# A two-layer attention kernel on one core: the first norm at other slots, its eps addition on GpSimd, and the minima transposed at full width

## The chip, the cores and the metric

The kernel runs on one NeuronCore of a Trainium2 chip. Times are device microseconds of one launch. The engines are TensorE (PE; PEld is its weight load), VectorE (DVE), ScalarE (ACT), GpSimd (POOL) and SyncE (SP), which here only issues DMAs. Each runs its own instruction list in order, and they meet at semaphores.

## What is computed

The reference is two cross-attention layers on x of 16 batches x 256 tokens x 256 features, which the kernel runs as three passes of attention:

```python
# layer 0 (pass 0)
tgt1 = _layer_norm(tgt, g1, be1)                       # eps 1e-5
tgt = tgt + _self_attn(tgt1, mask, ...)                # 16 heads of 16, additive mask
tgt = tgt + (memory @ Wg.T + bg)
tgt1 = _layer_norm(tgt, g2, be2)
x = tgt + (jax.nn.relu(tgt1 @ W1.T + b1) @ W2.T + b2)
# layer 1 (passes 1 and 2)
y = layer_norm(x, ln1_s, ln1_b)                        # eps 1e-6
x = mha(y, y, ..., causal=True) + x                    # pass 1
y = layer_norm(x, ln2_s, ln2_b)
y = mha(y, encoded, ..., causal=False) + x             # pass 2
z = layer_norm(y, ln3_s, ln3_b)
out = y + (jax.nn.relu(z @ mlp_w1 + mlp_b1) @ mlp_w2 + mlp_b2)
```

## The kernel before

A task is one batch in one pass; there are 48. The program is a software pipeline of steps; `steps` unrolls the edges of each pass and loops over pairs of steps within. In step s every engine goes through 16 slots (one for each head), and in each slot it does the parts of several tasks: `st.cur` (task s, whose scores are made), `st.prev`, `st.old` (earlier ones: output projection, MLP) and `st.nxt`, `st.nxt2` (later ones: q, k and v; the first norm). The order of an engine's work is that of the `if h == ...` lines in its `slot` function. Nothing else sets it, so an engine that waits in one place holds all that stands below.

The parts that matter here, for one step:

- **First norm** of the task two steps on: VectorE takes the statistics of `x_in` in slot 9 (L864), aggregates them and adds eps in slot 10 (L871, L874), GpSimd raises to the power -0.5 (L1095), VectorE normalises in slot 12 (L878), and TensorE transposes in slot 13 (L444).
- **q and k** of the next task are split into three bf16 parts. ScalarE writes the first part and the value (slots 3, 4), GpSimd subtracts (`q_f` slot 4, `k_f` slot 5; L1031 is the line of every subtraction), VectorE casts the second part (L914 slot 5, L917 slot 6), GpSimd makes the third (`q_part` slot 5, `k_part` slot 6). SP then writes the parts to DRAM (L381, L390) and reads them back as `q_stack` and `k_stack` (L399, L404). TensorE's score products of the next step need both stacks.
- **Scores.** TensorE makes the score product of head h in slot h (L494); it needs VectorE's guard of head h - 2. The guard (L858, in pass 2 L843) takes the minimum over the keys, and in passes 0 and 1 adds the bias on the way.
- **Minima** in passes 1 and 2: `top_split` on GpSimd splits the minima of four heads into bf16 parts (`top_part`, 12 columns), and TensorE transposes them with a 12-column weight at tile position (0, 96) (L521), in slots 2, 6, 10 and 14. ScalarE copies the rows into `q_stack` (L729), and `keyed_scores` (L542) uses them.
- **MLP** in passes 0 and 2, of task s - 2: four chunks of w1 on TensorE (slots 5 to 8), `h_f` on ScalarE (L805, slots 6 to 9), `h_hi` on VectorE (L921, slots 7 to 10), `h_lo` on GpSimd (slots 7 to 10). `h_f` of chunk 3 waits for `h_hi` and `h_lo` of chunk 1, that of chunk 4 for those of chunk 2. TensorE's V product (slot 10) waits for the last `h_f`, since it writes the same PSUM bank.
- **Norm of the attention output** (`rden`, `o_n`; L885, L890) in slot `NORM_AT` of VectorE, which is 6 in pass 0 and 10 in the others, then `o_f`, `ot_hi`, `ot_lo` one slot later.

In GpSimd's `slot` the power stands at the end of slot 10. Since eps is an immediate, the addition on VectorE is a `tensor_scalar`.

## Time and profile before

| | |
|---|---|
| median of 3 runs | 1709.86 us (1702.79 to 1710.65) |
| profiled execution | 1704.09 us, span 1702.3 us |
| mean granted TensorE clock | 0.956 |
| busy, share of the span | PE 86%, PEld 69%, DVE 71%, ACT 62%, POOL 49% |
| steady step of pass 0, of pass 2 | 38.5 to 40.1 us, 34.1 us |
| steps of pass 1 (766.90 to 1144.70) | 14 in 377.8 us |
| mean of one instruction | guard L858 0.42 (two for a head), copy of prob_t 0.68, h_lo 1.30, k_part subtraction 1.16, o_n 0.68, h_f 0.48 (two) |

A timeline row has the start, the duration, the engine, the line, the operation, what it writes and reads, and in brackets the idle time of that engine just before it and what ended it. "L494 PE" is line 494 of the kernel on TensorE.

### The profile page before, as it was taken

The numbers are of one execution on the slowest core, as the hardware profiler recorded it, in microseconds if no ns is written. First come the engines' busy times: TensorE is split into PE (matmuls) and PEld (weight loads), VectorE is DVE, ScalarE is ACT, GpSimd is POOL, SyncE is SP. The second block draws the span as 40 slices with busy tenths as digits, with TensorE's granted clock in tenths as the row PEclk, the third lists the DMA queues.
The fourth block names the chain that finished last, engine by engine and source line by source line (L and its number), as shares of the span: only waits on it lengthen the run. The fifth ranks groups of instructions, "written<-read, shape, count | busy, mean of one in ns | idle before, by whom it ended". The sixth has DMA issues, their size and how long they took to land.

```text
span 1702.3 us, 42833 instructions
## 1 busy us (share of the span) xinstructions
PE 1459.5 (86%) x13376; PEld 1175.9 (69%) x13376; DVE 1212.1 (71%) x3855; ACT 1061.9 (62%) x2153; POOL 834.7 (49%) x1125
## 2 busy tenths in 40 slices
PE   2789999999998998878787777778999999999986
PEld 1567788877777887765566555555777777777756
DVE  2688887888878887656666766666776777677742
ACT  3677676777777775445565555556656665666552
POOL 3345454444444566544344443444555655565533
PEclk8799999999999999989899999998999999999989
DMA  5645555444544455444655646574644364546300
GB/s 145 139 113 119 108 109 118 99 99 105 117 100 99 105 125 130 119 107 107 124 121 111 129 101 140 115 153 93 119 112 105 99 128 99 105 101 129 79 26 13
DMA packets 163511, 185.75 MB, mean 109 GB/s; under 512 B 15952, under 2 KB 140240, under 8 KB 163408
## 3 DMA queue, kind: packets, MB, share of 16 engines
q1 hardware_dynamic: 163408, 184.57, 49.8%
q8 instruction: 41, 0.67, 0.2%
q14 instruction: 62, 0.51, 0.1%
HBM read 125.78 MB, written 58.72 MB: 108 GB/s over the span
## 4 chain that ended last, share of the span: by engine, by line
PE 42%; issue 13%; ACT 12%; DVE 12%; DMA 9%; POOL 6%; SPq 5%; ACTq 1%; DVEq 0%; POOLq 0%
PE d_ps L437 16%; PE d_ps L673 8%; DMA k_stack<-parts 7%; PE o_ps L572 5%; PE s_ps L494 5%; PE t_ps L542 3%; DVE prob L858 3%; PE t_ps L508 3%; SPq L399 2%; DMA parts<-q_part 2%; ACT prob_t L721 2%; SPq L404 2%; DVE o_n L890 2%; POOL h_lo L1031 2%; PE m_ps L444 1%
## 5 line engine op out<-in xcount | busy, mean ns | idle before, releaser
L721 ACT ACTIVATE prob_t<-t_ps 128x384 f32<-128x384 f32 (+1 forms) x512 | 275.4, 551 | 393.0 <-PE t_ps L542 197.7
L494 PE MATMUL s_ps<-k_stack,q_stack 96*128 96x256 bf16 (+1 forms) x1536 | 294.6, 275 | 124.5 <-DMA k_stack<-parts 47.5
L712 ACT ACTIVATE prob<-prob,neg_max 128x256 f32<-128x256 f32 x512 | 233.8, 514 | 121.0 <-DVE neg_max L858 118.8
L494 PEld LDWEIGHTS s_ps<-k_stack,q_stack 96*128 96x128 bf16 x1536 | 115.1, 100 | 227.8 <-issue 65.7
L542 PE MATMUL t_ps<-q_stack,k_stack 108*128 108x256 bf16 (+1 forms) x1024 | 207.3, 269 | 23.0 <-ACT prob_t L721 14.3
L858 DVE CUSTOM_DVE_ANT_0 prob<-s_ps,bias_sb 128x256 f32<-128x256 f32 x512 | 192.4, 416 | 48.5 <-PE s_ps L494 36.7
L858 DVE CUSTOM_DVE_ANT_0 prob<-s_ps,causal 128x128 f32<-128x128 f32 (+1 forms) x512 | 158.5, 352 | 90.2 <-PE s_ps L494 88.0
L843 DVE TENSOR_REDUCE top<-s_ps 128x2 f32<-128x512 f32 x256 | 172.9, 682 | 54.8 <-PE s_ps L494 51.3
L1031 POOL TENSOR_TENSOR h_lo<-h_f,h_hi 128x512 fp32r<-128x512 f32 x128 | 165.9, 1296 | 86.6 <-DVE h_hi L921 86.6
L572 PE MATMUL o_ps<-prob_t,v_sb 128*17 128x256 f32 (+1 forms) x3072 | 200.7, 381 | 0.0
L437 PE MATMUL d_ps<-x2t_hi,w_hi 128*128 128x256 f32 x512 | 157.0, 307 | 38.2 <-ACT k_f L780 21.8
L901 DVE STREAM_TRANSPOSE o_q<-o_ps 128x256 f32<-128x256 f32 x192 | 86.1, 449 | 133.0 <-PE o_ps L572 131.4
L508 PE MATMUL t_ps<-ident_sb,prob 128*128 128x128 f32 x1024 | 160.3, 280 | 2.5 <-DVE prob_t L994 2.0
L673 PE MATMUL d_ps<-w_hi,h_hi 128*128 128x256 f32 x512 | 148.0, 289 | 4.4 <-POOL h_lo L1031 4.4
L673 PE MATMUL d_ps<-w_hi,h_lo 128*128 128x256 f32 x512 | 147.5, 288 | 0.0
L673 PE MATMUL d_ps<-w_lo,h_hi 128*128 128x256 f32 x512 | 146.4, 286 | 0.1
L437 PE MATMUL d_ps<-x2t_lo,w_hi 128*128 128x256 f32 x512 | 145.7, 285 | 0.0
L437 PE MATMUL d_ps<-x2t_hi,w_lo 128*128 128x256 f32 x512 | 145.4, 284 | 0.0
L729 ACT ACTIVATE q_stack<-o_ps 12x1024 bf16<-12x1024 f32 x128 | 130.1, 1016 | 11.5 <-PE o_ps L521 6.7
L437 PEld LDWEIGHTS d_ps<-x2t_hi,w_hi 128*128 128x128 f32 x512 | 98.8, 193 | 52.4 <-issue 44.1
L508 PEld LDWEIGHTS t_ps<-ident_sb,prob 128*128 128x128 f32 x1024 | 121.8, 144 | 14.0 <-issue 6.6
L1031 POOL TENSOR_TENSOR x2t_lo<-tf_b,x2t_hi 128x512 fp32r<-128x512 f32 x32 | 40.9, 1277 | 181.8 <-ACT tf_b L736 181.8
(115 smaller groups left out, 4063.5 us busy)
## 6 DMA issues: line engine op xcount, KB each, us to landing
q_stack<-parts SPq DMA_DIRECT2D x288, 128.0 KB, 4.0
k_stack<-parts SPq DMA_DIRECT2D x288, 128.0 KB, 6.4
parts<-q_part SPq DMA_DIRECT2D x96, 192.0 KB, 2.3
parts<-k_part SPq DMA_DIRECT2D x96, 192.0 KB, 2.3
ct_kept<-ct_hl SPq DMA_DIRECT2D x16, 512.0 KB, 8.0
x_in<-x_mid SPq DMA_DIRECT2D x32, 256.0 KB, 2.9
x_res<-x_mid SPq DMA_DIRECT2D x32, 256.0 KB, 3.0
ct_hl<-ct_kept SPq DMA_DIRECT2D x16, 512.0 KB, 8.2
```

The lines of the kernel that those rows point to most:

```text
L437: last = mm(dst, lhs, rhs, start=(opens and n == 0), stop=(closes and n == len(terms) - 1))
L494: last = mm(s_ps[:, h % 2, q * S:q * S + n], q_stack[0:ROWS, t.par, HEAD[h], q * P:(q + 1) * P], k_stack[0:ROWS, t.par, HEAD[h], 0:n], sta ...
L508: last = nc.tensor.transpose(t_ps[:, h % 2, c:c + P], prob[:, h % 4, q, k * P:(k + 1) * P], ident_sb[:, :])
L542: last = mm(t_ps[:, h % 2, k * S:k * S + S - lo], k_stack[:, t.par, HEAD[h], k * P:(k + 1) * P], q_stack[:, t.par, HEAD[h], lo:S], start=T ...
L572: last = mm(o_ps[32 * j:32 * j + VW, lo:S], v_sb[:, t.par, k, HEAD[h], :], prob_t[:, h % 8, k * S:k * S + S - lo], start=(k == 0), stop=(k ...
L673: last = mm(d_ps[:, 0, t * D:(t + 1) * D], lhs, rhs, start=(f == 0 and n == 0), stop=(f == FT - 1 and n == 2))
L712: last = nc.scalar.activation(prob[:, h % 4, q, :], prob[:, h % 4, q, :], ACT.Exp, bias=neg_max[:, h % 4, q:q + 1], scale=-1.0)
L721: nc.scalar.activation(prob_t[:, h % 8, 0:n], t_ps[:, h % 2, 0:n], ACT.Exp, scale=-1.0)\
L729: nc.scalar.activation(rows, o_ps[ROWS:ROWS + TOP, S:2 * S].unsqueeze(1).to_broadcast([TOP, CH, S]), ACT.Copy).then_inc(top_row.sem, 1)
L843: v.tensor_reduce(top[:, h // CH % 2, :, h % CH], s_ps[:, h % 2, :].rearrange("p (q k) -> p q k", q=TT), AX_X, ALU.min).then_inc(u_done.se ...
L858: last = v.tensor_tensor_reduce(prob[:, h % 4, q, 0:n], s_ps[:, h % 2, q * S:q * S + n], bias, 1.0, HUGE, ALU.add, ALU.min, least)
L1031: g.tensor_tensor(dst, a, b, ALU.subtract).then_inc(done, 1)
```

## The change

1. The statistics of the first norm go from slot 9 to slot 4, the aggregation from 10 to 5, and the normalisation from 12 to 6. The power on GpSimd goes with the aggregation, to the end of slot 5.
2. eps is added on GpSimd by a two-input addition against a tile of constants (`eps_sb`), for the first norm and the second. GpSimd waits for `ln_mv` (`ln2_mv`) in place of VectorE.
3. In pass 0 `NORM_AT` goes from 6 to 7.
4. The three parts of the minima are written to columns 96 to 107 of `top_wide`, whose other columns are zero, and transposed as a weight of 108 columns with no tile position.
5. The causal bias keeps one strip of 256 columns, from which both query tiles read a window.

```diff
-NORM_AT = (6, 10, 10)
+NORM_AT = (7, 10, 10)
+STATS_AT, MEAN_AT, HAT_AT = 4, 5, 6
...
-        top_part = sb("top_part", [P, 2, TT, CH, NSPLIT], BF16)
+        top_wide = sb("top_wide", [P, 2, TT, ROWS + TOP], BF16)
...
-                    last = mm(o_ps[ROWS:ROWS + TOP, S + q * P:S + (q + 1) * P],
-                              top_part[:, c % 2, q].rearrange("p j n -> p (j n)"), ident_bf[:, :],
-                              start=True, stop=True, tile_position=(0, ROWS))
+                    last = mm(o_ps[0:ROWS + TOP, S + q * P:S + (q + 1) * P], top_wide[:, c % 2, q, :], ident_bf[:, :],
+                              start=True, stop=True)
...
-                    bias = causal[:, q, 0:n] if t.p == 1 else bias_sb[:, t.par, q, 0:n]
+                    bias = causal[:, S - n:S] if t.p == 1 else bias_sb[:, t.par, q, 0:n]
...
                 last.then_inc(mv_done.sem, 1)
-                dve.wait_ge(mv_done.sem, mv_done.after(task))
-                v.tensor_scalar(ve_t[:, :], mv_t[:, :, 1], eps, None, ALU.add).then_inc(ve_done.sem, 1)
...
-                if h == 9 and has(st.nxt2):
+                if h == STATS_AT and has(st.nxt2):
...
-                if h == 10 and has(st.nxt2):
+                if h == MEAN_AT and has(st.nxt2):
...
-                if h == 12 and has(st.nxt2):
+                if h == HAT_AT and has(st.nxt2):
...
             g.memset(zeros[:, :, :], 0.0).then_inc(zeroed, 1)
-            pool.wait_ge(zeroed, 1)
+            g.memset(top_wide[:, :, :, :], 0.0).then_inc(zeroed, 1)
+            for p in range(NPASS):
+                g.memset(eps_sb[:, p], LN_EPS[p]).then_inc(zeroed, 1)
+            pool.wait_ge(zeroed, 2 + NPASS)
...
-                if h == 10 and has(st.nxt2):
+                if h == MEAN_AT and has(st.nxt2):
+                    pool.wait_ge(ln_mv.sem, ln_mv.after(st.nxt2))
+                    pool.sem_inc(passed, 1)
+                    g.tensor_tensor(ve[:, :], mv[:, :, 1], eps_sb[:, st.nxt2.p], ALU.add).then_inc(ln_ve.sem, 1)
...
                 if h == 14 and has(st.prev, MLP):
+                    pool.wait_ge(ln2_mv.sem, ln2_mv.after(st.prev))
+                    pool.sem_inc(passed, 1)
+                    g.tensor_tensor(ve2[:, :], mv2[:, :, 1], eps_sb[:, st.prev.p], ALU.add).then_inc(ln2_ve.sem, 1)
```

GpSimd in slots 5 to 8 of a step of pass 0, before (the names in brackets are the semaphores that an instruction waits for: `k_p2` counts VectorE's cast of k_part, `h_h` that of h_hi):

```order
L1031 TENSOR_TENSOR k_f<-k_f,k_part 128x512 [waits k_done]
L1031 TENSOR_TENSOR q_part<-q_f,q_part 128x512 [waits q_p2]
L1031 TENSOR_TENSOR k_part<-k_f,k_part 128x512 [waits k_p2]
L1074 REGISTER_ALU
L1031 TENSOR_TENSOR ct_hl<-tf_b,ct_hl 128x512 [waits ct_f]
L1078 REGISTER_ALU
L1031 TENSOR_TENSOR h_lo<-h_f,h_hi 128x512 [waits h_h]
```

and after:

```order
L1033 TENSOR_TENSOR k_f<-k_f,k_part 128x512 [waits k_done]
L1033 TENSOR_TENSOR q_part<-q_f,q_part 128x512 [waits q_p2]
L1095 REGISTER_ALU
L1097 TENSOR_TENSOR ve<-mv,eps_sb 128x2 [waits ln_mv]
L1101 TENSOR_TENSOR rstd<-ve,minus_half 128x2 [waits x_hat,ln_ve]
L1033 TENSOR_TENSOR k_part<-k_f,k_part 128x512 [waits k_p2]
L1077 REGISTER_ALU
L1033 TENSOR_TENSOR ct_hl<-tf_b,ct_hl 128x512 [waits ct_f]
```

The addition and the power now stand between the third parts of q and k.

VectorE in slots 5 to 7 of a step of pass 0, before (the ISA rows are guard 5, and below the cast guard 6):

```order
L914 CAST q_part<-q_f 128x512 [waits q_r]
L841 REGISTER_ALU
L858 ISA prob,neg_max<-s_ps,bias_sb 128x256 [waits s_mm,t_mm]
L858 ISA neg_max 128x1
L858 ISA prob,neg_max<-s_ps,bias_sb 128x256
L858 ISA neg_max 128x1
L885 RECIPROCAL rden<-o_q 128x32 [waits o_done]
L890 TENSOR_TENSOR o_n<-o_q,rden 128x2x8x16 [waits ot_f,rden_done]
L890 TENSOR_TENSOR o_n<-o_q,rden 128x2x8x16
L917 CAST k_part<-k_f 128x512 [waits k_r]
L841 REGISTER_ALU
L858 ISA prob,neg_max<-s_ps,bias_sb 128x256 [waits s_mm,t_mm]
```

and after, from the cast of k_part on:

```order
L916 CAST k_part<-k_f 128x512 [waits k_r]
L877 TENSOR_SCALAR x_in<-x_in,mv,rstd 128x256 [waits ln_rstd]
L877 TENSOR_SCALAR x_in<-x_in,mv,rstd 128x256
L842 REGISTER_ALU
L859 ISA prob,neg_max<-s_ps,bias_sb 128x256 [waits s_mm,t_mm]
L859 ISA neg_max 128x1
L859 ISA prob,neg_max<-s_ps,bias_sb 128x256
L859 ISA neg_max 128x1
L993 COPY prob_t<-t_ps 128x512 [waits t_mm]
L884 RECIPROCAL rden<-o_q 128x32 [waits o_done]
L889 TENSOR_TENSOR o_n<-o_q,rden 128x2x8x16 [waits ot_f,rden_done]
L889 TENSOR_TENSOR o_n<-o_q,rden 128x2x8x16
```

The normalisation, with its wait for `rstd`, stands ahead of guard 6, and the norm of the attention output behind it.

## Rows read from the trace of the kernel before

**Rows 1.** Stretches of one step, pass 0 and pass 2 (columns as in the first line).

```profile
core 0: us, PE busy (x) PEld busy (x) DVE busy (x) ACT busy (x) POOL busy (x), PEclk, DMA share, GB/s
461.50:500.00 38.50, 35.75 (x330) 31.08 (x328) 32.59 (x107) 28.43 (x67) 19.24 (x17) 1.00 0.53 109
1311.40:1345.50 34.10, 32.07 (x291) 25.41 (x290) 24.52 (x50) 21.88 (x42) 19.57 (x30) 1.00 0.41 108
```

**Rows 2.** Waits of TensorE in pass 1: total, times, longest.

```profile
PE s_ps L494 <- DMA k_stack<-parts: 35.2, 15, 4.4
```

**Rows 3.** Instructions that write `ve` or read it: ns min/median/max.

```profile
L874 DVE TENSOR_SCALAR ve<-mv x80: 169/170/1204, 8.5 to 1677.0; 128x2 f32<-128x2 f32 x80
L1095 POOL TENSOR_TENSOR rstd<-ve,minus_half x48: 688/690/708, 8.8 to 1573.9; 128x2 f32<-128x2 f32 x48
```

**Rows 4.** Timeline of GpSimd in a step of pass 0.

```profile
475.46 1.34 POOL L1031 TENSOR_TENSOR q_part<-q_f,q_part 128x512 bf16<-128x512 f32 x1
477.17 1.17 POOL L1031 TENSOR_TENSOR k_part<-k_f,k_part 128x512 bf16<-128x512 f32 x1 [0.37 <-DVE k_part L917]
478.29 1.30 POOL L1031 TENSOR_TENSOR ct_hl<-tf_b,ct_hl 128x512 fp32r<-128x512 f32 x1
```

**Rows 5.** Timeline of VectorE in the same step.

```profile
474.39 1.39 DVE L890 TENSOR_TENSOR o_n<-o_q,rden 128x256 f32<-128x256 f32 x1
475.70 1.39 DVE L917 CAST k_part<-k_f 128x512 bf16<-128x512 f32 x1
477.01 0.41 DVE L858 CUSTOM_DVE_ANT_0 prob<-s_ps,bias_sb 128x256 f32<-128x256 f32 x1
```

**Rows 6.** Timeline of GpSimd and VectorE at the end of that step.

```profile
499.49 1.27 POOL L1031 TENSOR_TENSOR xt_lo<-tf_a,xt_hi 128x512 fp32r<-128x512 f32 x1
...
500.17 1.07 DVE L878 TENSOR_SCALAR x_hat<-x,mv,rstd 128x256 f32<-128x256 f32 x2
```

**Rows 7.** Timeline of ScalarE in that step, the last h_f.

```profile
484.13 0.84 ACT L805 ACTIVATE h_f<-d_ps,cols_sb 128x256 f32<-128x256 f32 x2 [0.78 <-POOL h_lo L1031]
```

**Rows 8.** Timeline of TensorE in that step: score product 8, and V.

```profile
479.93 0.39 PE L494 MATMUL s_ps<-k_stack,q_stack 96*128 96x256 bf16 x2
...
485.02 0.38 PE L437 MATMUL d_ps<-w_hi,xt_hi 128*128 128x256 f32 x1 [0.45 <-ACT h_f L805]
```

**Rows 9.** Timeline of GpSimd in pass 1, a small addition.

```profile
994.51 0.20 POOL L1045 TENSOR_TENSOR top_rest<-top,top_part 128x8 f32<-128x8 f32 x1
```

**Rows 10.** Timeline of SP in the same step of pass 1.

```profile
994.37 0.93 SPq L390 DMA_DIRECT2D parts<-k_part  x2
995.71 2.66 SPq L399 DMA_DIRECT2D q_stack<-parts  x6
```

**Rows 11.** Timelines of four engines in a step of pass 2.

```profile
1322.07 1.37 DVE L914 CAST q_part<-q_f 128x512 bf16<-128x512 f32 x1 [1.03 <-POOL q_f L1031]
...
1324.88 0.68 DVE L843 TENSOR_REDUCE top<-s_ps 128x2 f32<-128x512 f32 x1
...
1325.04 1.16 POOL L1031 TENSOR_TENSOR k_part<-k_f,k_part 128x512 bf16<-128x512 f32 x1 [0.36 <-DVE k_part L917]
...
1330.45 0.84 ACT L805 ACTIVATE h_f<-d_ps,cols_sb 128x256 f32<-128x256 f32 x2
...
1336.49 0.39 PE L494 MATMUL s_ps<-k_stack,q_stack 96*128 96x256 bf16 x2 [0.40 <-DVE top L843]
```

**Rows 12.** Timeline of TensorE in that step, around a top product and V.

```profile
1331.05 0.39 PE L542 MATMUL t_ps<-q_stack,k_stack 108*128 108x256 bf16 x2
1331.27 0.38 PE L494 MATMUL s_ps<-k_stack,q_stack 96*128 96x256 bf16 x2
1331.59 0.28 PE L521 MATMUL o_ps<-ident_bf,top_part 128*12 128x128 bf16 x2
1331.79 0.39 PE L437 MATMUL d_ps<-w_hi,ct_hl 128*128 128x256 f32 x1
```

**Rows 13.** Weight loads by line: ns min/median/max.

```profile
L521 PEld LDWEIGHTS o_ps<-ident_bf,top_part x256: 83/87/93, 665.7 to 1651.6; 128*12 128x12 bf16 x128
L494 PEld LDWEIGHTS s_ps<-k_stack,q_stack x1536: 95/98/152, 41.3 to 1648.3; 96*128 96x128 bf16 x192
```

More of the change, by code:

```diff
@@ L176, in two_layers @@
         stats2, mv2, rstd2 = sb("stats2", [P, TT, 6]), sb("mv2", [P, TT, 2]), sb("rstd2", [P, TT])
+        eps_sb = sb("eps_sb", [P, NPASS, TT])
         ve, ve2 = sb("ve", [P, TT]), sb("ve2", [P, TT])
@@ L209, in two_layers @@
         bias_sb = sb("bias_sb", [P, 2, TT, S])
-        causal = sb("causal", [P, TT, S])
+        causal = sb("causal", [P, S])
         s_ps = es.enter_context(nc.psum_tensor("s_ps", [P, 2, 512], F32))
@@ L865, in statistics, with aggregate @@
                 last.then_inc(done.sem, 1)
-            def aggregate(task, st_t, mv_t, ve_t, eps, stats_done, mv_done, ve_done):
+            def aggregate(task, st_t, mv_t, stats_done, mv_done):
                 dve.wait_ge(stats_done.sem, stats_done.after(task))
@@ L936, in slot @@
                         dve.wait_ge(ln_rstd.sem, ln_rstd.after(st.nxt))
-                    aggregate(st.nxt2, stats, mv, ve, LN_EPS[st.nxt2.p], ln_stats, ln_mv, ln_ve)
+                    aggregate(st.nxt2, stats, mv, ln_stats, ln_mv)
                 if h == V_AT + 1 and has(st.nxt):
@@ L974, in slot @@
                         dve.wait_ge(ln2_rstd.sem, ln2_rstd.after(st.old))
-                    aggregate(t, stats2, mv2, ve2, LN_EPS[t.p], ln2_stats, ln2_mv, ln2_ve)
+                    aggregate(t, stats2, mv2, ln2_stats, ln2_mv)
                 if h == 15 and has(st.prev, MLP):
@@ L1010, in _ @@
             g.memset(minus_half[:, :], -0.5).then_inc(causal_made, 1)
-            g.memset(causal[:, :, :], 0.0).then_inc(causal_made, 1)
+            g.memset(causal[:, :], 0.0).then_inc(causal_made, 1)
             pool.wait_ge(causal_made, 2)
-            g.affine_select(out=causal[:, :, :], in_=causal[:, :, :], compare_op=ALU.is_ge, fill=MASKED, base=0,
-                            pattern=[[P, TT], [-1, S]], channel_multiplier=1).then_inc(causal_made, 1)
+            g.affine_select(out=causal[:, :], in_=causal[:, :], compare_op=ALU.is_ge, fill=MASKED, base=P,
+                            pattern=[[-1, S]], channel_multiplier=1).then_inc(causal_made, 1)
             g.memset(later[:, :], 0.0).then_inc(causal_made, 1)
@@ L1041, in top_split @@
                     pool.wait_ge(top_mm.sem, top_mm.after(before, cb + 1))
-                src, part = top[:, c % 2], top_part[:, c % 2]
+                src = top[:, c % 2]
+                part = top_wide[:, c % 2, :, ROWS:].rearrange("p q (j n) -> p q j n", n=NSPLIT)
                 g.tensor_tensor(part[:, :, :, 0], src, zeros[:, :, :], ALU.add).then_inc(top_1.sem, 1)
```

## The prediction

> **What bounds the kernel now.** I read the stretches first, then who waited for whom on TensorE, pass by pass, then the timelines of one step of each pass. One step is one task's 16 slots. A steady step of pass 0 lasts 38.5 us, TensorE being busy for 35.75 of them at full clock; one of pass 2 lasts 34.1 us with 32.07 busy [rows 1]. These two passes are TensorE's: what makes TensorE wait inside a step, after the middle of which it has no gap left to absorb it, lengthens the step. Pass 1 is another case: in 15 of its 16 steps TensorE's first score product waits until the stacks of the next task have landed [rows 2], 2.3 us on the mean. There a step is as long as the way from its start to the issue of the stack DMAs, plus the transfer. So three questions decide: does the change delay TensorE in passes 0 and 2, does it delay SP's issues in pass 1, and what do the full-width minima give back.
>
> **A row that prices the move: VectorE and GpSimd block one another.** The 2-element `ve` addition on VectorE takes 169 ns at least and 1204 at most [rows 3]. Its median is 170; 28 of the 80 instances are the long kind, and each of them starts while GpSimd runs one of its 1.28 us subtractions and ends when that ends. The same holds for the normalisation that the change moves: GpSimd's xt_lo runs from 499.49 to 500.76; x_hat's pair, issued at 500.17, ends at 501.24 [rows 6]. Of the 0.48 behind xt_lo's end I give 0.33 to the second, which leaves 0.15 for the first: it was held for the whole subtraction and ended just behind it. The k_part cast starts at 475.70 and ends at 477.09, 0.29 behind GpSimd's q_part [rows 4, 5]. And they take turns: o_n's second half (until 475.78), q_part, k_part's cast each end behind the one before. The score guards, which read PSUM, are not held.
>
> **The eps addition.** Removed from VectorE: 80 instructions, 28 x 1.20 + 52 x 0.17 = 42 us of busy time, of which the part on the path is the one in slot 10 of the steps of passes 0 and 2. In pass 2 it makes guard 10 late, and TensorE idles 0.40 us (at 1336.49) for it [rows 11]. Added on GpSimd: 80 two-input additions of 2 elements. Bounds: not below 0.1, not above the 0.69 of the power on the same shape [rows 3]; the nearest is the 8-element addition at 0.20 [rows 9], which I take, with 0.08 until the instruction that waits for it. For the second norm, at slot 14, the sum is nil: VectorE loses 0.17, GpSimd gains 0.28, ahead of the same power.
>
> **The first norm to slots 4 to 6.** Slot 4, two statistics (0.7 us): VectorE idles there for the scores in all three passes, and x_in has landed; nothing. Slot 5, two aggregates (0.24): guard 5 is later by that, and no one waits for it. On GpSimd, though, addition and power now stand between q_part's and k_part's subtractions: 0.28 + 0.69 = 0.97, less the 0.36 that it idled there for the k_part cast anyway [rows 11], gives k_part about 0.55 later. Slot 6 is the costly one. VectorE now waits, ahead of guard 6, for `rstd`. When the power ends, GpSimd's next instruction, k_part's subtraction, goes on at once, and VectorE, released only by a semaphore, loses the turn. So VectorE waits for power, then for a 1.16 us subtraction, and everything behind it on VectorE stands: guard 6, the copy of prob_t, h_hi for slot 7, which GpSimd (h_lo), then ScalarE (h_f, chunks 3 and 4) and TensorE (V) wait for.
>
> Pass 0, by the step from 461.5. Without the o_n that stood there, GpSimd's q_part ends near 476.5 instead of 476.80 [rows 4], the cast 0.29 later at 476.8, the addition at 476.9, the power at 477.65, k_part's subtraction at 478.8. The first normalisation ends at 478.95. GpSimd has ct_hl pending (it goes back to back now [rows 4]), so it takes its turn, 1.28, to 480.2, and the second normalisation ends at 480.35. Guard 6 stood at 477.01 [rows 5]; it is 3.3 us later. The norm of the attention output (rden, o_n), now in slot 7 of VectorE, comes between it and h_hi as it did before guard 6, so h_hi and h_lo are 3 us later. Score product 8 was issued at 479.93 [rows 8] and needs guard 6: at 481.0. ScalarE's exponentials of head 6 hold h_f 2, that holds TensorE's last w1 chunk (2.2 us late). The last h_f, which already waited 0.78 us for an h_lo and started at 484.13 [rows 7], waits for the second h_lo, which the same durations added up along VectorE and GpSimd put 2.5 later. V, which TensorE began at 485.02 after a gap of 0.45 [rows 8], then begins near 487.5. From there to the end TensorE has no gap: **+2.5 us a step**. What is removed in slots 9 to 12 of VectorE (0.7 + 0.24 + 1.2 + 1.07 us) comes too late to help, since V is already late. 14 steady steps give 35 us, the four steps at the pass's edges, with other neighbours, about 3.
>
> Pass 2, by the step from 1311.4. Guard 6, at 1324.88, comes 2.5 us later: k_part's subtraction, at 1325.04, goes to 1325.8 behind addition and power and ends at 1326.95; the two normalisations end 0.15 and 0.48 behind it, at 1327.4 (GpSimd's next needs h_hi, so there is one turn only). Guard 6 reaches score product 8 just in time. But h_hi is 1.9 later, and with it h_lo and the last h_f: it ran at 1330.45 and comes at 1332.3 [rows 11]; V began at 1331.79 [rows 12] and begins at 1333.2, +1.4. Given back: the wait before score product 12, 0.56 (0.40 in the row and the rest in the modelled end of the matmul before). Net +0.85.
>
> Pass 1. The q_stack issue at 995.71 follows the two k_part DMAs, issued at 994.37, 0.1 behind k_part's subtraction [rows 10]: +0.55. Guard 6 is also 2.3 us later, TensorE is about 1 us later at the end of a step, but there it idles 2.3 us on the mean for the stacks. So +0.55 a step.
>
> **The minima at full width.** Between a score product (a pair) and the top product TensorE's starts lie 0.32 apart, between t_ps and the score product, of the same size, 0.22; the top pair, with half the columns, is followed after 0.20 where 0.11 would do [rows 12]: about 0.1 us before and 0.1 behind each top product is lost to the change of tile position. I take 0.18 saved for each of 4 in a step. In pass 1 only the one in slot 2 lies on the way to the stacks: -0.18. In pass 2 those in slots 2 and 14 count, those between them are swallowed by the wait for V: -0.3. Weight loads: 12 columns take 87 ns, 96 columns 98 [rows 13], and they lie beside matmuls: nothing. By the Trainium skill (TensorE: Matmul & The Clock Gate, LDWEIGHTS) a load takes its columns divided by 1.2 in ns, so 108 columns would cost 80 ns more than 12; exposed in all 256, that would be an estimated 20 us more. By the rows the wider load takes 11 ns more, not 80.
>
> The two more memsets at the start (top_wide, eps) lie in GpSimd's wait for the constants: nothing. The causal tile changes its place, not its size in any instruction.
>
> **Sum.** Pass 0: +38. Pass 1: 16 x (0.55 - 0.18) = +6. Pass 2: 12 x (0.85 - 0.3) = +7, the last steps -0.5: together +51. The profiled execution took 1704.1 (span 1702.3), so 1755; the median of the runs shown is 5.8 higher and would give 1761. I predict **1757**.
>
> **Rivals.**
> (a) The second normalisation follows the first without giving up its turn. Then pass 0 costs 1.25 instead of 2.5 a step, and the sum is 1704 + 17 + 3 + 6 + 7 = 1737. Against it: the turns of rows 4 and 5.
> (b) Faster: `rstd` comes in time and the normalisation gets its turn before k_part's subtraction. This happens if VectorE, released by the power, is ahead of GpSimd's next instruction. Then guard 6 in pass 0 stands near 478.5, score product 8 has 1.4 us of slack, and what remains is the gain: V's gap of 0.45 in 14 steps (-6), in pass 2 0.56 and four switches of 0.18 (-1.3 x 13 = -17), pass 1 +6: 1704 - 17 = 1687. Against it: the q_part cast at 1322.07. It too was released by GpSimd (q_f), whose next instruction stood ready, and it took 1.37 where the undisturbed one takes 0.4 [rows 11].
> (c) No change: the delays are taken up by ScalarE's and VectorE's idle time in pass 0 (VectorE idles 2 us in slot 13) and the rest balances: 1700 to 1715. It needs h_lo not to be on V's path; the wait of the last h_f for h_lo speaks against that [rows 7].
> (d) Slower still: the wide weights' load, 98 ns [rows 13], no longer lies beside the score product but bare between it and the top product. All 256 would be 25 us: 1704 + 51 + 25 = 1780; those of pass 2 alone, 12: 1767. Against it: the t_ps and score products have loads as wide and lie 0.22 apart all the same [rows 12].
>
> **Chances.** Forecast (1740 to 1770) 0.50; (a) 0.15; partly absorbed, between (a) and no change, 0.08; (b) 0.14; (c) 0.08; (d) 0.05. What half a per cent (8.5 us) changes is about what a measurement of this kernel can tell from none. So slower 0.78, same 0.08, faster 0.14. The range leaves out (b) and the far end of (d): 1703 to 1772.
>
> **What would show it.** In the profile after: x_in's normalisations in slot 6 taking 1.2 us and more each in pass 0, one of them so in passes 1 and 2; guard 6 at 18.8 us of a pass 0 step; ScalarE's h_f waiting longer for h_lo; TensorE waiting some 2.5 us for h_f before V; pass 0 steps of 41 us, pass 2 steps of 34.5, pass 1's still ending on k_stack. L874's 1.2 us instances gone. The distance from score to top product 0.1 shorter. The forecast is wrong if the normalisations are 0.4 us long in slot 6, or if V's wait stays below 1 us.

## The result, and the profile after

The changed kernel takes **1756.87 us** (median of 4 runs, 1752.95 to 1758.52); the kernel before, run beside it, 1706.32 (4 runs, 1700.98 to 1710.65). The ratio is 1.0294, with a 95% interval of 1.0254 to 1.0334: slower by about 50 us. The profiled execution took 1757.15 us, its span is 1755.4, and the mean granted clock 0.938 where it was 0.956.

Where the time went, by stretches from the first score product of one step to that of another (a "step" here is one task, as in the prediction; 48 of them, 0 to 47):

| stretch | before | after | difference |
|---|---|---|---|
| start to the first score product | 41.3 | 45.3 | +4.0 |
| steps 0 to 15 (pass 0) | 613.6 | 646.3 | +32.7 |
| steps 16 to 18 | 112.0 | 114.1 | +2.1 |
| steps 19 to 32 (pass 1) | 377.8 | 383.8 | +6.0 |
| steps 33 to 45 (pass 2) | 438.7 | 446.3 | +7.6 |
| the rest | 118.9 | 119.5 | +0.6 |

Two of these differences, the start and pass 1, will turn out to lie within what two executions of one kernel differ by.

One step of pass 0 and one of pass 2 after, in the columns of [rows 1]; they were 38.50 and 34.10 us long:

```profile
486.20:527.00 40.80, 36.23 (x330) 30.82 (x329) 32.57 (x106) 28.58 (x68) 19.46 (x19) 1.00 0.45 103
1357.90:1392.70 34.80, 31.34 (x291) 25.52 (x290) 24.71 (x48) 21.84 (x41) 19.99 (x32) 1.00 0.42 105
```

TensorE does no more work in pass 0 (36.2 us busy instead of 35.8, partly the modelled ends of matmuls); it waits more. Slots 5 to 7 of that step on GpSimd, answering [rows 4]:

```profile
500.28 1.16 POOL L1033 TENSOR_TENSOR q_part<-q_f,q_part 128x512 bf16<-128x512 f32 x1
501.40 0.38 POOL L1097 TENSOR_TENSOR ve<-mv,eps_sb 128x2 f32<-128x2 f32 x1
501.86 0.69 POOL L1101 TENSOR_TENSOR rstd<-ve,minus_half 128x2 f32<-128x2 f32 x1
502.51 1.16 POOL L1033 TENSOR_TENSOR k_part<-k_f,k_part 128x512 bf16<-128x512 f32 x1
503.62 1.35 POOL L1033 TENSOR_TENSOR ct_hl<-tf_b,ct_hl 128x512 fp32r<-128x512 f32 x1
```

and on VectorE, answering [rows 5]:

```profile
500.36 1.37 DVE L916 CAST k_part<-k_f 128x512 bf16<-128x512 f32 x1 [1.37 <-POOL k_f L1033]
502.58 2.54 DVE L877 TENSOR_SCALAR x_in<-x_in,mv,rstd 128x256 f32<-128x256 f32 x2 [0.85 <-POOL rstd L1101]
505.04 0.41 DVE L859 CUSTOM_DVE_ANT_0 prob<-s_ps,bias_sb 128x256 f32<-128x256 f32 x1
...
507.38 0.42 DVE L920 CAST h_hi<-h_f 128x512 fp32r<-128x512 f32 x1
```

Read them together. The power ends at 502.55; VectorE starts the pair of normalisations at 502.58, GpSimd has started k_part's subtraction at 502.51, and the pair takes 2.54 us, until GpSimd's second subtraction is done as well. Guard 6 starts at 505.04, which is 18.84 us of the step (15.51 before), and h_hi at 21.2 (17.4 before). TensorE in the same step:

```profile
505.86 0.39 PE L496 MATMUL s_ps<-k_stack,q_stack 96*128 96x256 bf16 x2 [0.81 <-DVE neg_max L859]
506.56 0.63 PE L510 MATMUL t_ps<-ident_sb,prob 128*128 128x128 f32 x4 [0.30 <-DVE prob_t L993]
507.52 0.39 PE L439 MATMUL d_ps<-x2t_hi,w_hi 128*128 128x256 f32 x1 [0.34 <-ACT h_f L806]
...
512.20 0.39 PE L439 MATMUL d_ps<-w_hi,xt_hi 128*128 128x256 f32 x1 [0.34 <-ACT h_f L806]
```

The last row is V. It starts 26.0 us behind the step's first score product (at 486.24), 2.4 later than before (485.02 in [rows 8], of a step that starts at 461.48), but its own wait is 0.34. Most of the lateness was taken in the four small waits, 1.79 us together, where there had been one of 0.45. Over the whole program (ns, min/median/max):

```profile
L1097 POOL TENSOR_TENSOR ve<-mv,eps_sb x48: 194/375/391, 8.4 to 1614.6; 128x2 f32<-128x2 f32 x48
L1101 POOL TENSOR_TENSOR rstd<-ve,minus_half x48: 688/688/699, 8.6 to 1615.1; 128x2 f32<-128x2 f32 x48
L877 DVE TENSOR_SCALAR x_in<-x_in,mv,rstd x96: 400/1228/1385, 9.4 to 1617.0; 128x256 f32<-128x256 f32 x96
```

The 1204 ns instances of [rows 3] are gone, and the normalisations have become such instances: their median is 1228 ns. In pass 1 (steps 19 to 32) TensorE's longest waits have changed place (us in total, times, longest us). After:

```profile
PE s_ps L496 <- DVE top L859: 51.0, 26, 3.5
PE s_ps L496 <- DMA k_stack<-parts: 19.2, 11, 2.4
```

Before, in the same steps:

```profile
PE s_ps L494 <- DVE top L858: 33.6, 39, 1.1
PE s_ps L494 <- DMA k_stack<-parts: 29.0, 13, 4.4
```

### The profile page after: what moved, and what is told of

Same layout as the page of the kernel before. It is cut to its first block, busy times and chain, and to the rows that moved or that the text cites. A ratio compares the mean times of both kernels' runs of the same rounds, so it can differ in the third digit from the quotient of the medians.

```text
span 1755.4 us, 42898 instructions
## 1 busy us (share of the span) xinstructions
PE 1460.4 (83%) x13376; PEld 1194.6 (68%) x13376; DVE 1228.2 (70%) x3775; ACT 1062.2 (61%) x2153; POOL 850.3 (48%) x1209
## 4 chain that ended last, share of the span: by engine, by line
PE 33%; issue 22%; POOL 15%; DVE 12%; ACT 6%; DMA 6%; SPq 4%; DVEq 1%; POOLq 0%; ACTq 0%
PE d_ps L439 13%; PE d_ps L674 7%; DMA k_stack<-parts 6%; PE o_ps L573 4%; PE s_ps L496 4%; DVE prob L859 3%; PE t_ps L543 2%; POOL q_part L1033 2%; POOL q_f L1033 2%; PE t_ps L510 2%; SPq L401 2%; POOL k_part L1033 2%; DVE x_in L877 1%; SPq L406 1%; POOL rstd L1101 1%
## 5 line engine op out<-in xcount | busy, mean ns | idle before, releaser
L573 PE MATMUL o_ps<-prob_t,v_sb 128*17 128x256 f32 (+1 forms) x3072 | 207.7, 392 | 0.0
L806 ACT ACTIVATE h_f<-d_ps,cols_sb 128x256 f32<-128x256 f32 x256 | 107.6, 478 | 43.2 <-POOL h_lo L1033 32.8
```

The lines of the kernel that those rows point to most:

```text
L573: last = mm(o_ps[32 * j:32 * j + VW, lo:S], v_sb[:, t.par, k, HEAD[h], :], prob_t[:, h % 8, k * S:k * S + S - lo], start=(k == 0), stop=(k ...
```

## The experiments

The theory: the loss is VectorE's wait for `rstd` in slot 6, made longer by the turn that it loses to GpSimd's subtractions, and it reaches TensorE by h_hi, h_lo and h_f. The rivals: the additions on GpSimd, the power ahead of k_part's subtraction, guard 6 itself, the wide weight loads. All times of stages below are of steps 2 to 15 (pass 0), 19 to 32 (pass 1) and 33 to 45 (pass 2), each from one profiled execution. For the kernel before they are 547.0, 377.8 and 438.7; for the changed one 577.8, 383.8 and 446.3.

### Each part alone

**Minima at full width**, on the kernel before, together with the causal strip, which makes the room for the wide tile:

```diff
-                              top_part[:, c % 2, q].rearrange("p j n -> p (j n)"), ident_bf[:, :],
-                              start=True, stop=True, tile_position=(0, ROWS))
+                    last = mm(o_ps[0:ROWS + TOP, S + q * P:S + (q + 1) * P], top_wide[:, c % 2, q, :], ident_bf[:, :],
+                              start=True, stop=True)
```

> The kernel before with the minima at full width and the causal strip (parts 4 and 5 of the change), nothing else. My theory (the loss lies in the first norm's place, the wide minima give a little): the distance from score product to top product falls from 0.32 to 0.22 us and the one behind it from 0.20 to 0.11; pass 2 steps 0.3 shorter, pass 1 steps 0.2, start-up as before at 41.3 us; total 6 to 8 us less, ratio 0.996. Rival (the wider weight load lies bare): 3 to 20 us more, ratio 1.002 to 1.012. Rival for the 4 us that the start-up lost: if it is the memset of the wide tile on GpSimd, the first score product comes 1 us or more later here.

Ratio 0.9986 (0.9956 to 1.0017). The saving itself is there and is the size that was forecast: the median distance from the score product's last start to the top product's first fell from 200 to 109 ns, and from the top product's last start to the next matmul from 149 to 28, together 0.21 us, four times a step. The steps of pass 2 did not follow: 436.9 instead of 438.7. TensorE's waits in pass 2 (us in total, times, longest us) show where it went. This variant:

```profile
PE t_ps L541 <- ACT prob_t L720: 10.9, 11, 1.0
PE s_ps L494 <- DVE top L842: 10.3, 16, 1.2
...
PE d_ps L437 <- ACT h_f L804: 3.9, 12, 0.3
```

The kernel before, the same stretch:

```profile
PE t_ps L542 <- ACT prob_t L721: 8.2, 11, 0.7
PE s_ps L494 <- DVE top L843: 6.2, 14, 1.1
```

TensorE arrives earlier and waits longer, for `prob_t`, for `top`, and for h_f, where it had not waited at all: 10.7 us more, of 13 x 0.84 = 10.9 saved. The saving was on TensorE's time, but TensorE's time there was not the bound to the last 0.2 us. Which of the two made it, the tile position that is gone or the weight that has grown from 12 to 108 columns, this run doesn't separate: it changes both.

**eps on GpSimd alone**, the norm at its old slots:

```diff
-                v.tensor_scalar(ve_t[:, :], mv_t[:, :, 1], eps, None, ALU.add).then_inc(ve_done.sem, 1)
+                    g.tensor_tensor(ve[:, :], mv[:, :, 1], eps_sb[:, st.nxt2.p], ALU.add).then_inc(ln_ve.sem, 1)
```

> The kernel before with eps added on GpSimd for both norms (part 2), the first norm at slots 9, 10 and 12 as before. My theory: in pass 2 the wait before score product 12 goes (0.4 us of gap, 0.56 with the matmul's end), steps 34.1 to 33.6; pass 0 and pass 1 as before; total 6 to 8 us less, ratio 0.996. Rival (the 0.37 us that an addition took on GpSimd in the changed kernel is its price everywhere, and delays the last h_lo or x_hat): no gain, ratio 0.999 to 1.003, pass 0 steps up to 0.3 longer.

Ratio 0.9991 (0.9953 to 1.0030). Pass 2 is 429.6 us, 9.1 less: a step 33.25 instead of 33.96, and TensorE's wait for `top` falls from 6.2 to 3.0 us. Pass 0 is 544.8, unchanged or a little less; an addition on GpSimd takes 194 ns at the median here, not 375. Pass 1 is 392.7, 15 us more than in the trace of before. Whether that is the addition's doing, a second trace of the kernel before has to say (below: it is not). Then a gain of 9.1 us, a ratio of 0.995, should show in the whole, and the interval just leaves it out; why it does is open.

**The move alone** (first norm at 4, 5, 6, attention norm at 7; eps on VectorE, minima as before):

```diff
-NORM_AT = (6, 10, 10)
+NORM_AT = (7, 10, 10)
+STATS_AT, MEAN_AT, HAT_AT = 4, 5, 6
```

> The kernel before with the first norm at slots 4, 5 and 6 and the attention norm at 7 in pass 0 (parts 1 and 3), eps still on VectorE, minima as before. My theory (this part alone is the loss): pass 0 steps 2.2 to 3 us longer, pass 2 steps 1.2 longer (0.7 of the changed kernel and what the wide minima gave back), pass 1 0.6 to 0.9 longer, first score product at 45 instead of 41.3 us; total 60 to 75 us more than before, ratio 1.035 to 1.044, above that of the whole change. Rival (parts of the loss come from GpSimd's additions standing ahead of the power): less than the whole change, ratio 1.015 to 1.025.

Ratio 1.0213 (1.0157 to 1.0269). Stages 571.8, 382.7 and 447.4: the loss is here. But my sum for this kernel (60 to 75 us) was wrong, since I added back gains that do not add: 35 us were measured, and the ratio is within the rival's 1.015 to 1.025. In pass 2 the step is 34.82 against 34.74 of the whole change: once the norm has left slots 10 to 12, eps on GpSimd has almost nothing left to give, because both buy the same wait before score product 12. In pass 0 this kernel is even 6 us faster than the whole change. There `rstd` is ready at 15.85 us of a step and not at 16.30: on VectorE the addition doesn't stand behind q_part's subtraction in GpSimd's list. Beside the move, eps on GpSimd costs 0.43 us a step in pass 0.

**All but the move** (changed kernel, slots 9, 10, 12 and 6):

> The changed kernel with the first norm back at slots 9, 10 and 12 and the attention norm at 6: parts 2, 4 and 5 together. My theory: the gains of the two add, 12 to 15 us less than before (ratio 0.992), pass 2 steps 33.3, start-up at 41.3 us. Rival (both buy the same slack): no better than the better one alone, ratio 0.996. Rival for the start-up: 45 us here too if the memsets cause it.

Ratio 0.9926 (0.9894 to 0.9958). Stages 547.3, 389.2, 427.9, a pass 2 step 33.15: the two gains add to 10.8 us in pass 2, nearly all of it from eps. It is the base for what the move costs: pass 0 577.8 - 547.3 = 30.5 us (2.2 a step), pass 2 446.3 - 427.9 = 18.4 (34.74 - 33.15 = 1.6 in a steady step).

### What in slot 6 is dear

**Give VectorE its turn**: GpSimd starts k_part's subtraction only behind the normalisation.

```diff
                     pool.wait_ge(k_p2.sem, k_p2.after(st.nxt))
+                    if has(st.nxt2):
+                        pool.wait_ge(x_hat.sem, x_hat.after(st.nxt2))
                     sub(k_part[:, 2], k_f[:, :, :], k_part[:, 1], k_p3.sem)
```

> The changed kernel with one wait more: in slot 6 GpSimd starts k_part's subtraction only when VectorE has normalised x_in, so the normalisation gets its turn. If the lost turn is what makes the move dear (my theory): the pair of normalisations in slot 6 takes 0.8 us instead of 2.5, guard 6 of a pass 0 step stands near 17.2 us of the step instead of 18.8, V at most 1 us later than before instead of 2.5, pass 0 steps 39.3 to 39.8 (40.8 with the changed kernel), pass 2 steps 34.0 to 34.4 (34.7), pass 1 0.8 a step longer since k_part comes later; total 10 to 20 us below the changed kernel, ratio to before 1.015 to 1.022. Rival (the wait for the power itself is the price, the turn is not): pass 0 steps 40.5 or more, ratio 1.028 to 1.035.

Ratio 1.0339 (1.0299 to 1.0378). Timeline of the same place in a step of pass 0 that starts at 478.6:

```profile
494.98 0.74 DVE L877 TENSOR_SCALAR x_in<-x_in,mv,rstd 128x256 f32<-128x256 f32 x2 [0.85 <-POOL rstd L1103]
...
497.30 1.58 DVE L889 TENSOR_TENSOR o_n<-o_q,rden 128x256 f32<-128x256 f32 x2
```

The pair takes 0.74 us instead of 2.54, and guard 6 stands at 17.0 us of the step, as expected. V comes at 24.99 (median of the odd steps) where it came at 25.95 with the change and at 23.55 before. So of the 2.40 us of V's lateness the lost turn is 0.96, not all; 0.8 us of what was won at the normalisation is lost again at the attention norm (`o_n`, 1.58 us here, 0.76 with the change), which now meets the subtraction; and 1.44 stays. That is not the wait for the power alone (0.85) but also the 0.74 that the pair itself takes ahead of h_hi. Pass 0 took 562.0, between the two. In pass 2 the turn is worth 0.1 a step (34.61). Pass 1 was 426.5, 43 us more than with the change, where I had expected 13; this is taken up below. (The traced execution, 1786.47 us, is the longest of five; the others took 1770.64 to 1776.65.)

**Guard 6 first**, then the normalisation:

> The changed kernel with the normalisation behind guard 6 instead of ahead of it; it is still ahead of slot 7. If the delay reaches TensorE by h_hi, h_lo and h_f (my theory): TensorE's wait of 0.8 us before score product 8 goes, guard 6 stands near 15.6 us of the step, but h_hi is as late as before, V comes at most 0.5 us earlier, pass 0 steps 40.2 to 40.8; ratio 1.024 to 1.029. Rival (guard 6 and the exponentials behind it carry the delay): V comes 1.5 us earlier or more, pass 0 steps below 39.6, ratio below 1.018.

Ratio 1.0246 (1.0207 to 1.0286).

```profile
494.38 0.42 DVE L859 CUSTOM_DVE_ANT_0 prob<-s_ps,bias_sb 128x256 f32<-128x256 f32 x1 [0.69 <-PE s_ps L496]
...
495.08 2.00 DVE L877 TENSOR_SCALAR x_in<-x_in,mv,rstd 128x256 f32<-128x256 f32 x2
```

Guard 6 is as early as before the change: 15.42 us in the median of the odd steps, 15.54 before. (In the step of the rows, which starts at 478.2, it waited 0.69 us for a score product that came late.) The wait of 0.8 us ahead of score product 8 is gone; h_hi comes 0.66 earlier, V 0.67 (expected 0.5 at most), pass 0 is 565.9. So guard 6's place is 0.67 of V's 2.40 us, and the larger part is what stands behind the normalisation whichever way the two are put. Pass 2 gains too (a step 34.18 instead of 34.74). That the whole is no shorter is pass 1, 400.6 us here and 383.8 with the change.

**Addition and power behind k_part's subtraction**:

> The changed kernel with GpSimd's addition and power behind k_part's subtraction in place of ahead of it. k_part's subtraction comes 0.8 us earlier, which in pass 1 shortens the way to the stacks; the power ends at about 17.4 us of a pass 0 step instead of 16.35, and the normalisation then meets ct_hl's subtraction in place of k_part's. My theory: guard 6 at 19 to 20 us, pass 0 steps as with the changed kernel or up to 0.6 longer, pass 2 (which has no ct_hl) steps 0 to 0.5 shorter, pass 1 0.4 to 0.8 a step shorter; total within 8 us of the changed kernel, ratio 1.022 to 1.032. Rival (addition and power ahead of k_part's subtraction are the price): ratio below 1.015.

Ratio 1.0346 (1.0307 to 1.0385), worse than the change, and outside what I had expected.

```profile
509.51 1.68 DVE L877 TENSOR_SCALAR x_in<-x_in,mv,rstd 128x256 f32<-128x256 f32 x2 [2.20 <-POOL rstd L1083]
```

VectorE idles 2.20 us for the power instead of 0.85, then loses only one turn. `rstd` comes 1.34 us later, h_hi 0.5, V 0.48, and a step is 0.6 longer on the mean; pass 2 steps are 35.25, 0.5 longer, where I had them shorter. k_part's own 0.7 us (15.55 instead of 16.26) bought nothing in pass 1 (383.7 against 383.8). In the changed kernel the power ahead of k_part's subtraction isn't the price; when `rstd` comes is.

**Only the normalisation back in slot 12**, statistics, addition and power staying in slots 4 and 5:

```diff
-STATS_AT, MEAN_AT, HAT_AT = 4, 5, 6
+STATS_AT, MEAN_AT, HAT_AT = 4, 5, 12
```

> The changed kernel with the normalisation alone back in slot 12; statistics, aggregation, addition and power stay in slots 4 and 5, the attention norm in 7. My theory (VectorE's wait in slot 6 is the price, the early statistics and power cost next to nothing): guard 6 near 15.6 us of a pass 0 step, pass 0 steps 38.6 to 39.0, pass 2 steps 33.1 to 33.6, k_part's subtraction 0.55 later which costs pass 1 at most 0.5 a step; ratio 0.993 to 1.000. Rival (the power in slot 5, ahead of k_part's subtraction, or the attention norm in slot 7 carries the loss): pass 0 steps 39.6 or more, ratio above 1.01.

Pass 0 is 546.5 us, as before the change, with V at 23.86 (23.77 in the variant without the move): all of pass 0's loss is the normalisation in slot 6, its wait and its turn, and neither the early power nor the attention norm in slot 7 has a share that can be seen. Pass 2 steps are 33.63, half a microsecond above the variant with everything late (33.15); k_part's subtraction is late there, but no run separates the early power from the early statistics. The ratio, 1.0106 (1.0063 to 1.0149), is where the rival had it. Pass 0 is not as the rival said, but pass 1 is 405.4, and there the rival's cause has its part, as the sums of the next section show: the power in slot 5 is free in pass 0 and not in pass 1.

One distance ties these runs together. In pass 0 V starts 4.81 to 4.83 us behind the first h_hi in most steps of every kernel with the attention norm in slot 7, and never less than 4.80. Medians of the odd steps:

| | h_hi | V |
|---|---|---|
| before | 17.45 | 23.55 |
| normalisation back in slot 12 | 19.05 | 23.86 |
| its turn given | 20.18 | 24.99 |
| guard 6 first | 20.46 | 25.28 |
| move alone | 20.68 | 25.50 |
| the change | 21.12 | 25.95 |
| power behind k_part | 21.62 | 26.43 |

Before the change 6.10 us lie between them, so h_hi had 1.3 us to spare, and only what goes beyond that reaches V.

### Pass 1 and the clock

**The kernel before, once more**, unchanged:

> The kernel before, unchanged, profiled a second time. Two stretches of the experiments differ from the trace of before though nothing there was edited alike: the start (first score product at 45.0 to 46.5 us in the changed kernel and in all of its variants, 41.3 before) and pass 1. If these belong to one execution and not to a kernel: the first score product at 45 us or later here too, and steps 19 to 32 at 380 to 395 us, not 377.8. Rival (the loss of 4 us at the start is the change's): 41.3 us again, within 0.5.

1723.67 us. The first score product came at 45.5, passes 0 and 2 took 546.8 and 438.9 (0.2 from the first trace), and pass 1 392.8: 15.0 us more than in the first trace. Steps 19 to 32 as one stretch, kernel before in the first trace, then again (columns as in [rows 1]; the clock is the third number from the end):

```profile
766.90:1144.70 377.80, 298.51 (x3062) 220.35 (x3062) 253.00 (x1144) 216.04 (x392) 162.50 (x325) 0.93 0.59 121
```

```profile
770.40:1163.20 392.80, 305.22 (x3063) 223.15 (x3064) 253.49 (x1144) 216.30 (x392) 163.39 (x327) 0.90 0.60 116
```

So the +4.0 at the start isn't the change's, and no difference in pass 1 of less than some 15 us between two traces says anything. One thing that differs is the clock: 6 of the 14 steps begin their first 4 us at 0.65 of it or less in the first trace, 10 in the second. Two starts of pass 1 steps in the first trace, both fully busy:

```profile
1008.90:1012.90 4.00, 3.99 (x47) 3.11 (x48) 2.24 (x13) 2.00 (x3) 0.42 (x2) 1.00 0.54 156
1061.00:1065.00 4.00, 4.00 (x33) 2.12 (x33) 1.86 (x10) 0.98 (x2) 0.00 (x0) 0.50 0.27 91
```

At 1.00 (2.4 GHz) TensorE gets 47 matmuls done in 4 us, at 0.50 (1.2 GHz) 33. The first start came behind a wait of 1.82 us for the stacks, the second behind one of 4.40. The products for q and k lie in these microseconds, so the stacks go out later: in the first trace the q_part DMAs are issued at 10.4 to 11.2 us of the eight steps that start at 1.00, and at 11.9 to 13.2 of the six others, which are 1.1 us longer on the mean. In the variant with the normalisation at 12 every step starts low (none issues q before 11.5 us); here is the start of one, behind 5.40 us of waiting:

```profile
967.70:971.70 4.00, 3.96 (x34) 2.60 (x35) 1.78 (x10) 0.98 (x2) 0.00 (x0) 0.53 0.26 89
```

(the variant that gives VectorE its turn is the same in this: no step issues q before 11.6 us). The waits of the former for the stacks in steps 19 to 32 are (us, times, longest)

```profile
PE s_ps L496 <- DMA k_stack<-parts: 75.1, 15, 6.3
```

By the Trainium skill (TensorE: Matmul & The Clock Gate, What's actually happening) "the default state is throttled, and activity releases the throttle"; the rows agree: 1.00 behind 1.82 us of idleness, 0.50 behind 4.40. The length of the wait alone doesn't tell, though: one step started at 0.50 behind 2.21 us, another at 1.00 behind 2.47.

The clock is not all of it. In each trace the steps 19 to 32 can be added up from four parts: from the step's start to the issue of q_part's DMAs, from there to the last issue of k_stack, from there to its landing, and what is left until TensorE starts the next step. Sums over the 14 steps, in us (a low start is one whose first 4 us have 0.7 of the clock or less):

| | low starts | to q's issue | to the last issue | to the landing | left |
|---|---|---|---|---|---|
| before, first trace | 6 | 160.8 | 112.5 | 103.2 | 1.4 |
| before, again | 10 | 167.4 | 111.6 | 112.4 | 1.4 |
| all but the move | 13 | 167.4 | 112.6 | 107.8 | 1.4 |
| normalisation at 12 | 14 | 172.9 | 121.7 | 109.3 | 1.4 |
| the change | 1 | 153.8 | 119.6 | 104.5 | 5.8 |
| its turn given | 14 | 173.6 | 133.5 | 118.0 | 1.4 |
| all but the move, 28 products (below) | 1 | 147.2 | 110.8 | 113.0 | 5.8 |

Of the 15.0 us between the two traces of before, 6.6 are the later q, where the clock acts, and 9.2 are longer transfers, whose cause is open. The normalisation at 12 has 16.2 us more than all but the move: 9.1 are k_part's subtraction behind the addition and the power, which SP waits for ahead of the stacks, and 5.5 the later q. And of the 43 us by which the turn's variant exceeds the change, 13.9 are k_part behind the normalisation (13 had been expected), 19.8 the later q and 13.5 longer transfers, less 4.4 in the last column.

It is tempting to say that a long wait breeds the next. From step to step the first trace doesn't show it: TensorE's wait at the end of a step that started low is 1.75 us on the mean, of the others 2.34, since TensorE's own work ends later as well.

To test the clock, TensorE was given work of no use ahead of the wait: products of 256 columns into the score bank, overwritten by the real one, in the 15 later steps of pass 1, on the variant without the move. The wait for the stacks, which stood first in the step, now stands behind them and behind the wait for the guard. If a long idle stretch ahead of a step lowers the clock of its start, filling it should bring q out earlier.

```diff
+                    if t.p == 1 and not t.first:
+                        for _ in range(WARM):
+                            mm(s_ps[:, 0, 0:S], ident_bf[0:ROWS, :], k_stack[0:ROWS, 1 - t.par, HEAD[0], :],
+                               start=True, stop=True)
                     pe.wait_ge(stacked.of(t), stacked.after(t))
```

> Parts 2, 4 and 5 of the change on the kernel before (slots 9, 10, 12), and in the 15 later steps of pass 1 TensorE makes 16 products of 256 columns with no use (1.7 us) into the score bank ahead of its wait for the stacks. [...] If so, the products shorten the idle stretch, the granted clock stays at 1.00 at the start of the steps, the q_part DMAs go out at 10.4 instead of 11.7 to 13 us of the step, and steps 19 to 32 take 365 to 380 us instead of 389; total 10 to 20 us below the variant without them, ratio to before 0.982 to 0.988. Rival (the transfer alone sets the step, the clock is a bystander): 389 within 5 us, ratio 0.992.

> The same with 28 such products (3.0 us). By the theory of the clock: the clock at the start of the steps stays up in all of them, and where the stacks land sooner than 3 us after TensorE's last product the surplus costs up to 1 us a step; steps 19 to 32 at 368 to 382 us, ratio 0.982 to 0.990, about the same as with 16 or 3 to 5 us more. Rival: 389 us or more, since the products only add work ahead of the score product, ratio 0.992 to 1.000.

With 16 the ratio is 0.9877 (0.9819 to 0.9935), pass 1 385.2: the clock was low at the start of 9 of 14 steps still, and five issued q before 10.6 us. With 28 it is **0.9854 (0.9804 to 0.9904)**, 1693.47 us, pass 1 376.8, and q went out before 10.6 us in 13 of 14 steps, all but the first of pass 2, which has no such products. Pass 1 and one step's start, with 28:

```profile
771.00:1147.80 376.80, 319.20 (x3400) 252.28 (x3397) 248.19 (x1130) 216.54 (x392) 166.96 (x340) 0.95 0.63 121
...
797.00:801.00 4.00, 4.00 (x49) 3.19 (x48) 2.24 (x13) 2.00 (x3) 0.38 (x2) 1.00 0.42 126
```

and the waits for the stacks in that stretch:

```profile
PE s_ps L501 <- DMA k_stack<-parts: 11.0, 7, 5.3
```

TensorE does 337 matmuls more, and pass 1 is 12 us shorter than without them (389.2). Without them no step issued q before 11.2 us. By the table q goes out 20.2 us sooner in sum, and 9.6 come back as longer transfers and as time left to TensorE. So the clock at the start is a cause of when q goes out, and not a bystander. What the products give the whole is less sure: the first trace of before had 377.8 us without any, and the intervals of the ratios with them and without (0.9804 to 0.9904, 0.9894 to 0.9958) touch. This version, parts 2, 4 and 5 of the change with the 28 products, has the lowest ratio of all, 1.5% below the kernel before.

**The same products in the changed kernel**, to see what the move costs pass 1 once the clock at the start is out of the way:

> The changed kernel with the 28 products of no use ahead of the wait for the stacks in pass 1. What is open is what the change costs in pass 1, where its slower engines meet a slower clock. Theory: with the norm in slot 6 TensorE ends its step 1 to 2 us later and idles 2.4 us at most for the stacks, so 3.0 us of products do not fit in any more: the clock stays at 1.00 at the start of the steps, as in the variant without the move, but the steps are TensorE's and not the stacks': waits for k_stack nearly gone, steps 19 to 32 at 385 to 405 us, 10 to 25 above the 376.8 of the variant without the move; ratio to before 1.025 to 1.040. Rival (the move costs pass 1 nothing but the 0.65 us at k_part): steps 19 to 32 at 376 to 386 us, ratio 1.015 to 1.024.

Ratio 1.0293 (1.0249 to 1.0336), pass 1 394.0: 17.2 us above 376.8, or 1.2 a step, and 10 more than the changed kernel without them.

```profile
806.40:1200.40 394.00, 327.65 (x3400) 258.74 (x3398) 264.05 (x1130) 215.97 (x392) 165.94 (x336) 0.90 0.58 116
```

```profile
PE s_ps L501 <- DVE top L864: 52.2, 29, 3.5
...
PE s_ps L501 <- DMA k_stack<-parts: 3.1, 1, 3.1
```

The steps are no longer the stacks' but TensorE's, and its wait is the one ahead of score product 8, for guard 6: 3.2 to 3.5 us in each of the 14 steps, with the products and without, where it was 1.1 at most before. In the changed kernel that wait is followed by half the clock, as this stretch of the step that starts at 859.8 shows beside the start of another:

```profile
874.90:878.90 4.00, 4.00 (x33) 2.64 (x34) 2.50 (x14) 1.00 (x3) 0.84 (x4) 0.50 1.05 237
998.80:1002.80 4.00, 4.00 (x47) 3.18 (x48) 2.23 (x13) 2.00 (x3) 0.74 (x4) 1.00 0.46 131
```

So in pass 1 the change moved the long idle stretch, and the low clock behind it, from the start of the step, where it delays the stacks, to the middle, where the DMAs of k_part are already out. What it costs there no run isolates. At the start, 13 of 14 steps keep their clock, and 8 issue q before 10.6 us, 3 in either trace of before. By the table, beside the first trace of before, q goes out 7.0 us sooner in sum, the last issue comes 7.1 later behind it, the transfers take 1.3 and what is left 4.4 more. So the trace shows +6 only.

## Why the prediction was right, and where not

The prediction was 1757; 1756.87 was measured, and the slower side had 0.78. That it is right to 0.2 us is luck: the terms missed by 3 us in pass 0, the start's 4 us were not in the sum, and pass 1 agrees by chance. Step by step:

- **The wait in slot 6 and the lost turn.** Right, and to the tenth: guard 6 at 18.8 us was forecast, 18.84 measured; V 2.5 later was forecast, 2.4 measured; both normalisations were held, each by its own subtraction. In between, h_hi was forecast 3 us later and is 3.7; it had 1.3 to spare, which brings V back to 2.4. A step of pass 0 is 2.2 longer and not 2.5, since TensorE regains 0.2 behind V. The term of 38 measured 32.7 and part of the 2.1 of steps 16 to 18.
- **Where TensorE waits.** Wrong. One wait of 2.5 us ahead of V was forecast, and a wait below 1 us named as the sign of a wrong forecast; it is 0.34. The lateness is in four waits of 0.81, 0.30, 0.34 and 0.34 us, since each thing that TensorE needs (guard 6, the copy of prob_t, two h_f) was late by a similar amount. The time of V was the thing to forecast, not its gap.
- **The share of the turn.** The text leaned on the turn. It is 0.96 of 2.40 us in pass 0 and 0.1 of 1.6 in pass 2. The larger part is the plain wait for a power that ends 0.85 us after VectorE is free, and the pair's own 0.74 us ahead of h_hi.
- **eps on GpSimd.** 0.20 a piece was taken between bounds of 0.1 and 0.69; in slot 5, beside VectorE's cast of k_part, it is 0.38, elsewhere 0.19. In pass 0 it costs 0.43 a step, because it stands behind q_part's subtraction: a queue that the sum didn't charge.
- **Pass 2.** +0.85 - 0.3 = +0.55 a step was forecast, 0.78 measured. The gross price of the move was forecast as 1.4 ahead of V and is 1.6. Given back are 0.8, as forecast, but by other hands: 0.7 is the wait that goes from score product 12, which eps on GpSimd removes as well as the move does, and the four full-width minima, for which 0.3 was taken, give 0.1.
- **Pass 1.** +6 was forecast from 0.55 lost at k_part and 0.18 won at the top product, and +6.0 stands in the table. This is agreement by chance. The same kernel differs by 15 us there from one execution to the next, and the trade between a sooner q and later stacks, with two low clocks in it, is one that the prediction did not see, though [rows 2] had waits of 2.3 us on the mean and 4.4 at most. The price of k_part itself was right, by a path read wrongly: the q_stack issue of [rows 10] did not follow k_part's DMAs but the landing of q_part's, as the chain through that step has it (start, us, what):

```profile
993.27 2.35 DMA parts<-q_part
995.66 0.06 issue
995.71 0.32 SPq L399
```

It is so in all 14 steps. k_part's DMAs were only 0.1 us short of that; with the change they are behind it, and the q_stack issue comes 3.44 us behind q's where it came 2.87 behind it: 0.57 later, 0.55 forecast.
- **The start.** No cost was forecast; the 4.0 us in the trace are there in the kernel before as well.
- **Rival (d).** The wide weight load takes 128 ns at the median and not 98, and still lies beside matmuls: the distances on both sides of the top product fell. Rivals (b) and (c) fell with the normalisations' 1228 ns and with V. Rival (a), one turn instead of two, isn't what happened in pass 0; in pass 2 there was one turn, as forecast.

So the terms of passes 0 and 2 stand within 0.3 us a step: 38 forecast and 34.8 measured for steps 0 to 18, 7 and 7.6 for pass 2. The 6 of pass 1 only looks confirmed. How much of the 50 us is pass 1's stays open within the spread of its executions; of the rest, 43 us are in the table's steps 0 to 18 and 33 to 47.

## What to carry to other kernels

A producer's last small step on another engine (here a 0.69 us power) sets where its consumer may stand in an in-order list: put the consumer behind the point at which the result is there anyway, or it holds everything below it, and beside a neighbour that blocks SBUF, it also loses its place to whatever that neighbour does next. The small step has a price as well where it is put early: ahead of k_part's subtraction it added 9 us to pass 1's way to the stacks and nothing to pass 0. When a gain in one engine's busy time brings nothing, compare the waits behind it and not the busy times: 10.7 of 10.9 us came back as longer waits. And where a step ends in a wait for a transfer, look at TensorE's granted clock just behind that wait; with work of no use ahead of it 14 steps took 377 us here instead of 389. Before two traces are compared, take one of the kernel before twice.

## What was not expected of the hardware

- An idle stretch of TensorE costs more than itself: behind 4.40 us of waiting TensorE did 33 matmuls in 4 us, behind 1.82 us 47. In the first trace the steps that start low issue q 1.8 us later on the mean and are 1.1 longer. One and the same kernel took 378 and 393 us for 14 steps; 6.6 of these 15 us are the later q, 9.2 longer transfers.
- VectorE and GpSimd, released within 0.1 us of one another, did not share: the pair of normalisations took 2.54 us beside two subtractions (1.16 and 1.35) and 0.74 with GpSimd held off. The block then found another victim (`o_n`, 0.76 to 1.58). By the Trainium skill (SBUF — State Buffer, Who interferes with whom) it is an exclusive lock and "whoever issues first gets the shared pair for the whole instruction"; the trace agrees for the first half of the pair, and shows besides that the one that waited comes next, and then waits again.
- Taking the tile position away from the 12-column top product, and widening it to 108 columns, saved 0.09 us ahead of it and 0.12 behind it, although the weight load grew from 87 to 128 ns.
